# Five PSUM banks in turn for the scores of three attention streams, with the shared products moved into the transposes' two banks

## The reference, cut to what matters

```
S = q_h k_h^T (+ mask);  P = exp(S - max(S));  out_h = (P v_h) / sum(P);  x += concat(out) Wp + bias
```

## Time and profile before

| what | value |
|---|---|
| median of 3 runs | 2754.14 us (2752.77 to 2756.01) |
| the profiled execution's own time | 2750.36 us |
| its span, first to last instruction | 2748.6 us |
| busy: PE, PE weight load | 2386.5 us (87%), 1706.0 us (62%) |
| busy: DVE, ACT | 1222.7 us (44%), 1013.9 us (37%) |
| stream ra, about | 157 to 430 us |
| stream ca, about | 465 to 815 us |
| stream ma, about | 2091 to 2280 us |

### The profile page before, as it was taken

The page is one execution under the profiler, slowest core; times in us unless marked ns, Lnnn a source line. Parts: engine busy times, 40 slices in busy tenths (PEclk is TensorE's granted clock), DMA queues, the critical chain, the costliest instruction groups (busy, mean ns, idle before and its releaser), DMA issues. The chain is left out here.

```text
span 2748.6 us, 38901 instructions
## 1 busy us (share of the span) xinstructions
PE 2386.5 (87%) x15301; PEld 1706.0 (62%) x15301; DVE 1222.7 (44%) x2353; ACT 1013.9 (37%) x2866; POOL 146.0 (5%) x238
## 2 busy tenths in 40 slices
PE   6778887999988999989999999978998997874894
PEld 4455655666655666666666666656876765654773
DVE  5456665777764434333333333345344443331003
ACT  3245564777762111113333333343223443331122
POOL 0000000000000000000000000021001000002003
PEclk8989999999999999999999999999999999996996
DMA  3000001000002000020000000000001000012332
GB/s 113 16 1 1 1 1 39 13 24 13 24 11 82 1 1 0 1 109 8 8 9 9 8 9 1 1 28 1 0 25 57 16 9 16 1 57 75 115 119 65
DMA packets 52535, 74.82 MB, mean 27 GB/s; under 512 B 8051, under 2 KB 41349, under 8 KB 51205
## 3 DMA queue, kind: packets, MB, share of 16 engines
q1 hardware_dynamic: 50820, 68.14, 7.4%
q0 software_dynamic: 1536, 4.20, 0.6%
HBM read 63.94 MB, written 8.39 MB: 26 GB/s over the span
## 5 line engine op out<-in xcount | busy, mean ns | idle before, releaser
L856 ACT ACTIVATE ca_prob<-bank,ca_nmax 128x512 f32<-128x512 f32 x256 | 174.0, 690 | 93.1 <-DVE ca_nmax L922 93.1
L922 DVE TENSOR_REDUCE ca_nmax<-bank 128x1 f32<-128x512 f32 x256 | 164.2, 683 | 56.3 <-PE bank L714 56.2
L856 ACT ACTIVATE na_prob<-bank,na_nmax 128x257 f32<-128x257 f32 x256 | 117.9, 473 | 180.9 <-DVE na_nmax L922 180.9
L1446 PE MATMUL bank<-XN,rf_W 128*128 128x512 f32 x384 | 171.8, 598 | 0.0
L1457 PE MATMUL bank<-rf_W,rf_h 128*128 128x256 f32 x768 | 170.8, 379 | 0.0
L1457 PEld LDWEIGHTS bank<-rf_W,rf_h 128*128 128x128 f32 x768 | 145.9, 190 | 33.1 <-issue 14.8
L728 PEld LDWEIGHTS bank<-cst,ca_prob 128*128 128x128 f32 x1024 | 112.3, 142 | 73.7 <-issue 63.3
L856 ACT ACTIVATE ra_prob<-bank,ra_nmax 128x256 f32<-128x256 f32 x256 | 118.2, 482 | 104.1 <-DVE ra_nmax L922 104.1
L1501 ACT ACTIVATE rf_r<-bank 128x512 f32<-128x512 f32 x96 | 57.4, 598 | 255.3 <-PE bank L1446 255.3
L728 PE MATMUL bank<-cst,ca_prob 128*128 128x128 f32 x1024 | 140.5, 279 | 6.6 <-DVE ca_pT L928 5.9
L922 DVE TENSOR_REDUCE na_nmax<-bank 128x1 f32<-128x257 f32 x256 | 90.8, 417 | 118.2 <-PE bank L714 118.2
(11 more groups left out here) (399 smaller groups left out, 4505.8 us busy)
## 6 DMA issues: line engine op xcount, KB each, us to landing
xl_w<-in_L_ffn_w SPq DMA_DIRECT2D x16, 1024.0 KB
dp_cx<-in_ctx_tok SPq DMA_DIRECT2D x4, 1024.0 KB, 14.8
ca_v<-in_ctx_values SPq DMA_DIRECT2D x8, 512.0 KB, 4.5
rf_W<-in_L_ffn_w SPq DMA_DIRECT2D x8, 512.0 KB, 8.7
na_Wkv<-in_L_xattn_Wkv SPq DMA_DIRECT2D x1, 4096.0 KB
na_cxT<-in_ctx SPq DMA_DIRECT2D x8, 512.0 KB, 3.4
ma_cxT<-in_ctx SPq DMA_DIRECT2D x8, 512.0 KB, 3.4
X<-in_x SPq DMA_DIRECT2D x1, 2048.0 KB, 7.6
```

The costliest lines, as they stand in the source:

```text
L856: e = act.activation(prob[:, n % 2, u, hh * keys:(hh + 1) * keys], S[u][:, hh * keys:(hh + 1) * keys], ACT.Exp, bias=nmax[:, n % 2, u, hh: ...
L922: v.tensor_reduce(nmax[:, n % 2, u], S[u][:, 0:W].rearrange("p (h k) -> p h k", h=per), AX.X, ALU.max, negate=True).then_inc(maxed, 1)
L1446: mm = pe.matmul(g.bank[n % 3][:], W1[:, k, c * P:(c + 1) * P], g.XN[:, k, gi * GT:(gi + 1) * GT], start=(k == 0), stop=(k == KD - 1))
```

## The change

In streams of four groups the scores take banks 0, 1, 2, 3 and 6 in turn (unit 4n+u takes the bank of number (4n+u) mod 5), so a unit waits for the exponential five units back in place of four. The shared products no longer have a bank of their own: they and the transposes are put into one list, `ring`, in the order in which PE issues them, and take banks 4 and 5 in turn. Each one, turn or shared product, waits until the entry two before it in the list has been read out of its bank (`wait_ring`). The order on the engines is not touched. Streams of two groups and the products ahead of a stream's first iteration keep their banks and waits.

```diff
+    FIVE = GA == 4
-    S = [g.bank[u] for u in range(4)]
+    S = [g.bank[u] for u in (range(4) if not FIVE else (0, 1, 2, 3, 6))]
...
+    ring = []
+    for n in range(NR + 3):
+        ring += slots[n][0]
+        ring += [("turn", n - 1, f) for f in range(2) if 1 <= n <= NR]
+        if not values_due(n):
+            ring += slots[n][1]
+        ring += [("turn", n - 1, f) for f in range(2, FILLS) if 1 <= n <= NR]
+        if values_due(n):
+            ring += slots[n][1]
+        ring += slots[n][2]
+    ring_at = {use: i for i, use in enumerate(ring)}
+
+    def score_bank(n, u):
+        return S[(4 * n + u) % len(S)]
+
+    def turn_bank(n, f):
+        return TB[ring_at[("turn", n, f)] % 2] if FIVE else TB[f % 2]
...
-        return g.bank[n % 4] if n < len(first) else M
+        if n < len(first):
+            return g.bank[n % 4]
+        return TB[ring_at[use] % 2] if FIVE else M
+
+    def wait_ring(pe, use):
+        if ring_at[use] < 2:
+            return
+        last = ring[ring_at[use] - 2]
+        if last[0] == "turn":
+            pe.wait_ge(copied_v if last[2] % 2 == 0 else copied_a, (FILLS * last[1] + last[2]) // 2 + 1)
+        else:
+            wait_freed(pe, last)
...
-                        if n > 0:
-                            pe.wait_ge(exped, 4 * (n - 1) + u + 1)
+                        if 4 * n + u >= len(S):
+                            pe.wait_ge(exped, 4 * n + u - len(S) + 1)
...
-                if fill >= 2:
+                if FIVE:
+                    wait_ring(pe, ("turn", n, f))
+                elif fill >= 2:
                     pe.wait_ge(copied_v if f % 2 == 0 else copied_a, (fill - 2) // 2 + 1)
...
-                before = ready_at[use] - 1 - (4 if ready_at[use] <= len(first) else 1)
-                if before >= (0 if ready_at[use] <= len(first) else len(first)):
-                    wait_freed(pe, order[before])
+                if FIVE and ready_at[use] > len(first):
+                    wait_ring(pe, use)
+                else:
+                    before = ready_at[use] - 1 - (4 if ready_at[use] <= len(first) else 1)
+                    if before >= (0 if ready_at[use] <= len(first) else len(first)):
+                        wait_freed(pe, order[before])
```

More of the change, by code:

```diff
@@ L590, in attention_stream @@
     ld = [g.sem(f"{tag}_loaded{j}") for j in range(2)] if n_loads else None
-    S = [g.bank[u] for u in range(4)]
+    FIVE = GA == 4
+    S = [g.bank[u] for u in (range(4) if not FIVE else (0, 1, 2, 3, 6))]
     TB = [g.bank[4], g.bank[5]]
     M, O = g.bank[6], g.bank[7]
+    assert not FIVE or FILLS == 4
     INV = 2 if reg is not None else 1
@@ L705, in scores @@
                         i, a, hs = unit(n, u)
-                        if n > 0:
-                            pe.wait_ge(exped, 4 * (n - 1) + u + 1)
+                        if 4 * n + u >= len(S):
+                            pe.wait_ge(exped, 4 * n + u - len(S) + 1)
                         if mask is not None:
                             ml, mr = mask(i, b, hs)
-                            pe.matmul(S[u][:, 0:W], ml, mr, start=True, stop=False, skip_group_check=True)
+                            pe.matmul(score_bank(n, u)[:, 0:W], ml, mr, start=True, stop=False, skip_group_check=True)
                     for hh in range(per):
@@ L713, in scores @@
                             i, a, hs = unit(n, u)
-                            mm = pe.matmul(S[u][:, hh * keys:(hh + 1) * keys], q_of(hs[hh], i, b), k_of(hs[hh], i, b),
+                            mm = pe.matmul(score_bank(n, u)[:, hh * keys:(hh + 1) * keys], q_of(hs[hh], i, b), k_of(hs[hh], i, b),
                                            start=(mask is None), stop=(hh == per - 1), skip_group_check=True)
@@ L727, in turn @@
                     c0 = (blk // KC) * keys + (blk % KC) * P
-                    mm = pe.transpose(TB[f % 2][:, j * P:(j + 1) * P], prob[:, n % 2, u, c0:c0 + P], ident)
+                    mm = pe.transpose(turn_bank(n, f)[:, j * P:(j + 1) * P], prob[:, n % 2, u, c0:c0 + P], ident)
                 mm.then_inc(turned, 1)
@@ L856, in exps @@
                     e = act.activation(prob[:, n % 2, u, hh * keys:(hh + 1) * keys],
-                                       S[u][:, hh * keys:(hh + 1) * keys], ACT.Exp, bias=nmax[:, n % 2, u, hh:hh + 1],
+                                       score_bank(n, u)[:, hh * keys:(hh + 1) * keys], ACT.Exp, bias=nmax[:, n % 2, u, hh:hh + 1],
                                        accum_out=sums[:, f % 2, i, hl:hl + 1])
@@ L863, in copy_turned @@
                 o = pT[:, n // 2 % 2, 4 * f:4 * f + 4, n % 2] if GA == 4 else pT[:, n % 2, :, f]
-                act.activation(o, TB[f % 2][:].rearrange("p (j q) -> p j q", j=4), ACT.Copy).then_inc(copied_a, 1)
+                act.activation(o, turn_bank(n, f)[:].rearrange("p (j q) -> p j q", j=4), ACT.Copy).then_inc(copied_a, 1)
             def shared(use):
@@ L921, in maxima @@
                 v.wait_ge(scored, 4 * n + u + 1)
-                v.tensor_reduce(nmax[:, n % 2, u], S[u][:, 0:W].rearrange("p (h k) -> p h k", h=per),
+                v.tensor_reduce(nmax[:, n % 2, u], score_bank(n, u)[:, 0:W].rearrange("p (h k) -> p h k", h=per),
                                 AX.X, ALU.max, negate=True).then_inc(maxed, 1)
@@ L927, in copy_turned @@
                 o = pT[:, n // 2 % 2, 4 * f:4 * f + 4, n % 2] if GA == 4 else pT[:, n % 2, :, f]
-                v.tensor_copy(o, TB[f % 2][:].rearrange("p (j q) -> p j q", j=4)).then_inc(copied_v, 1)
+                v.tensor_copy(o, turn_bank(n, f)[:].rearrange("p (j q) -> p j q", j=4)).then_inc(copied_v, 1)
             def invert(f):
```

## The result

The changed kernel takes 2807.64 us (median of 4 runs, 2805.73 to 2811.25) against 2753.45 us before (2751.29 to 2756.01): a ratio of 1.0198, 95% interval 1.0180 to 1.0216. It is slower by 54 us. The forecast was 2816 us in a range of 2790 to 2838.

A forecast was written before the change was run, and what follows sets the result against it. PE was taken as the engine with least slack, waiting 25.2 us for exponentials in ca. Losses from the ring, net of the fifth bank, 37 (ca) + 18 (ra) + 7 (ma) = 62 us, gave 2816 us, range 2790 to 2838.

The forecast's parts named there:

- The chain: In ca's even iterations, copy of turn 0, product, take, turn 3 and scores would run serially; ca +37 us in sum.
- odd: Odd iterations of ca without a product would gain their wait for the exponentials, 0.22 us each, 24 times.
- the prediction's paragraph on the clock: A full ca sample would grow 5.85 us, all PE idle, to 8.7 of 48.9 us; no clock fall expected.
- the walk: Step-by-step timing of single iterations in ca, ra and ma: +37, +18 and +7 us, 62 in all; chance 0.73.
- queries, keys, values and projection come seven times inside the stream: In ca, the four products' growths of 1.95, 1.17, 1.37 and 1.43 us, charged seven times: 41.4 us.
- The link of 0.14 us: Time assumed from the end of a take to PE's start, 299.85 to 299.99 in ra; also used behind copies.
- iteration 2: In ra, turn 1 waits for the keys' take, delaying projection, its take, copy of turn 2 and reg 2: +1.27 us.
- ma: Stream of two iterations a sample: even +1.45 us, odd -0.40; seven samples of +1.05, +7 us.
- Faster: Rival: the ring's waits are all met in time and five banks pay in ca: 2729 us, chance 0.06.
- Only ca pays: Rival: in ra and ma two banks give back what the ring takes, leaving ca's loss: 2791 us, chance 0.12.
- the row behind that rival: In ra and ma, shared products already queue on one another for bank 6, waits of 1.18 to 1.35 us.
- The clock: Rival: a tenth of ca's PE work runs at the 1.2 GHz level, 32 us in all: 2848 us, chance 0.06.

The follow-up runs named there:

- e4: Changed kernel with ScalarE copying the keys of ca once more into a spare tile: keys iteration 6.43 to 6.91 or 6.92 us, ca 370.53 to 373.99.
- e6: Changed kernel with VectorE in ca copying turn 0 right after the maxima of unit 0: 2805.41 us, ratio 1.0199 to the kernel before.
- e2: Changed kernel with scores on four banks and bank 6 as third bank of the list: 2739.63 us, ratio 0.9947 to the kernel before.
- e1: Changed kernel with scores back on four banks, bank 6 idle, the list of two banks kept: 2818.21 us, ratio 1.0224 to the kernel before.
- e5: Kernel before the change with ScalarE copying the keys of ca once more into a spare tile: ca 339.08 us against 339.14.
- e3: The change made in stream ca alone, ra and ma as before: 2782.56 us, ratio 1.0106 to the kernel before.

## Why the prediction was right, point by point

**The chain was named rightly and in ca sized within 0.1 us.** Forecast growth of an iteration, and measured in the fourth sample: queries 1.95 and 1.98, keys 1.17 and 1.16, values 1.37 and 1.32, projection 1.43 and 1.41, spread 0.59 and 0.61, odd -0.22 and -0.29. A full sample was to take 48.9 us and takes 48.66. The growth is not all PE idle, as the prediction's paragraph on the clock has it: idle rose to 6.95 us and not to 8.7, since PE's listed busy time rose too, by 1.55 us. e4 shows that the take is in the chain, e6 that the copy is, e2 that both go with one more bank in the list.

**The edges of ca were mis-sized**, and they are most of the 5.6 us by which ca came out shorter. The whole first sample shrank by 1.76 us (43.08 to 41.32), where the walk gives 1.95 + 1.17 + 1.37 - 0.71 - 3 x 0.22 = +3.12: 4.9 us. Of these, 2.6 are the queries: the step "queries, keys, values and projection come seven times inside the stream" charged them in the first sample too, but in iteration 0 no turn has been issued yet, so there is nothing in the list to wait for, and it shrank from 4.81 to 4.15 us. Another 1.4 are iteration 3, which ran at the lower clock before and not after; the walk had no term for that. And 0.7 is iteration 1, which carries no spread in the first sample and got no gain in the walk.

**The link of 0.14 us was misread, and too long for products.** It was read from the end of the exponential of reg 0's take at 299.85. But that take has a second instruction on ScalarE, which the prediction overlooked:

```profile
299.74 0.20 ACT L872 ACTIVATION_READ_ACCUMULATOR ra_rp<-bank,ra_rst 80x1 f32 x1
```

It ends at 299.94, and the product starts 0.05 us behind it, at 299.99. A product behind a copy likewise starts 0.05 us after it (646.12 in ca); the transposes do take 0.14 (648.75 to 648.89). In ca the short link is made up for by a turn that takes 0.56 us to the next scores, where I put 0.5; that the sum comes out within 0.1 us is in this part luck. In ra the link is not made up for. The timeline after of iteration 2 of a ra sample, answering to the first three of the earlier trace rows:

```profile
320.04 0.61 ACT L1324 ACTIVATE ra_k<-bank 128x512 f32<-128x512 f32 x1
...
320.79 0.63 PE L764 MATMUL bank<-cst,ra_prob 128*128 128x128 f32 x4 [1.07 <-ACT ra_k L1324]
...
321.25 1.89 PE L1287 MATMUL bank<-ra_outT,ra_Wp 128*128 128x256 f32 x8
...
323.18 0.88 DVE L1300 SCALAR_TENSOR_TENSOR X<-bank,ra_bias,X 128x256 f32<-128x256 f32 x2 [1.55 <-PE bank L1287]
...
323.98 0.68 DVE L967 COPY ra_pT<-bank 128x512 f32<-128x512 f32 x1
...
324.20 0.63 PE L764 MATMUL bank<-cst,ra_prob 128*128 128x128 f32 x4 [0.62 <-DVE X L1300]
...
324.71 1.09 PE L845 MATMUL bank<-ra_v,ra_rpT 128*80 128x256 f32 x4
```

Every step is the forecast's: turn 1 behind the keys' take, the projection, its take, the copy of turn 2, reg 2. But the projection's take starts 1.93 us after the product (2.03 where the product itself had to wait), and reg 2 starts 0.05 us after the copy's end at 324.66. So iteration 2 grew by 1.06 and not 1.27 us; the others by 0.46 (forecast 0.5), -0.48 (-0.41) and 0.98 (1.08). A full sample grew by 2.02 in place of 2.44 us; the first one shrank by 0.75, again by its iteration 0 (10.08 to 7.72 us). Reg 0 and the queries are the first two of the list there, so the queries' product waits for nothing, where before it waited 1.11 us for the take of reg 0; and it is listed with 2.51 us in place of 3.55, against 1.99 in a full sample, as the granted clock stood at 0.50 for a part of it in both.

**ma** came within a microsecond, in part by luck: a full sample grew by 0.71 in place of 1.05, mostly by the same link, and the last one, where the projection is the only product in the way, grew by 2.02, for which the walk had no term of its own.

**The rivals.** *Faster*: the score wait did go, 25.2 to 1.1 us, but the odd and the empty iterations alone kept the gain, 13.2 us by e1 (10.6 without the falls of the clock) where the walk had 8. *Only ca pays*: ra and ma lose 20.3 us together; yet the row behind that rival was a good one, since the waits on bank 6 that it pointed at are where e2 wins: ra and ma together are 19.7 us shorter with one bank more. *The clock*: 1.00 in the windows of the full samples and in ca of the kernel after as a whole, so this rival falls. The Trainium skill's TensorE: Matmul & The Clock Gate, "A second HAM failure mode: psum-queue depth-cycling", is not borne out in these windows: with 14% of a sample idle in gaps of up to 1.2 us in the rows above the clock stayed at the 2.4 GHz level. But the clock was not quite out of it. In the first sample of ra it fell for some microseconds in every trace, and in ca it fell in all four traces with four score banks (before, e1, e2, e5) and in none of the four with five (after, e3, e4, e6). In the kernel before, PE idled 1.00 and then 0.71 us, the wait for the exponentials, in each of the two iterations ahead of the fall; with the fifth bank that second gap is gone. That the gap is the cause was not tested. The rule of the Trainium skill's Perfetto Trace Analysis, "Optimization Strategy", that a gap which repeats can mean too little PSUM, is borne out in a wider sense than I used it: PSUM was short, but at the list more than at the scores.

**The range.** Two of its numbers do not follow from the prediction's own terms: 2816 with 15 more or 10 less is 2806 to 2831 and not 2803 to 2832, and half of the way from 2816 to the clock's 2848 is 2832 and not 2838. The result, 2807.64, lies inside either.

**What stays open.** Of 55.3 us that the span grew, 3.6 lie outside the distances from first to last scores. Of these, 2.0 belong to the change: behind the last scores the stream still has turns and products to work off, and from there to the next stage's first product it is 19.41 us in place of 18.87 in ra and 24.96 in place of 23.53 in ma (17.40 and 17.41 in ca), and ma's is 24.96 or 24.97 in e1, e4 and e6 as well. The walk had no term of its own for this. The other 1.6 I take for scatter of single executions: between ma's last scores and the end, for one, the kernel before takes 484.24 us and e3, with the same instructions there, 480.91. In e1 the span grew by 73.4 us and the streams by 65.7, in e3 by 31.5 and 31.3.

## What to carry to other kernels

Before giving a bank to the stage that waits most, ask what the bank buys at each place: here 11 to 13 us at the scores, where the next thing in PE's order was nearly due anyway, and some 44 us in ca at the shared products, where it kept product, copy and take side by side. My rule from this, shown for this kernel only: where one engine works through a list in order and others empty its banks, a pool should hold the entry in flight, the one being read out, and any whose reader is queued behind other work; with one bank less, the readers' work joins the engine's own chain. And walk the first and last rounds on their own: most of the error in ca lay there.

## What the runs showed of the hardware that I had not expected

- PE starts 0.05 us after a copy has ended when the product of the keys waits for it (646.07 to 646.12), and 0.14 us when a transpose waits for a take (648.75 to 648.89). In the full samples of ra, ca and ma, before and after, shared products start 0.05 or 0.06 us behind the read-out that their row names, of VectorE or ScalarE alike; ca's scores and, but for two rows, the transposes start 0.14 or 0.15 us behind it.
- Two copies of one bank in a row on ScalarE start 0.49 us apart (0.47 in e5), though each is listed with 0.59 to 0.63 us: the listed end lies behind the next start, and in e4 the added copy cost 0.49 us and not its duration.
- A listed wait of 0.22 us on PE before the scores was worth 0.29 us when it went (5.27 to 4.98).
